# Cross-attention and a LoRA mixture on one core: the context's means through device memory, scores in 512-column matmuls, and the fifth tile turned by TensorE

## What is computed

```python
# _layernorm: (x - mean) / sqrt(var + 1e-5)
scores  = einsum('bsd,bmd->bsm', layernorm(x), ctx) / 32       # 64 context rows per batch
attn    = softmax(where(mask, scores, -1e30))
x       = x + einsum('bsm,bmd->bsd', attn, ctx)                # zero where no row is valid
n       = layernorm(x)
base    = n @ weight.T                                         # 1024 x 1024
probs   = softmax(n @ router_w.T)                              # 8 experts; the two best, renormed
expert  = sum over e of w[e] * ((n @ lora_A[e].T) @ lora_B[e]) * 2   # rank 16
x       = x + base + expert
```

## Time and profile before

| | |
|---|---|
| median of 3 runs | 1054.0 us (1053.96 to 1054.96) |
| the profiled execution's own time | 1054.39 us |
| its span, first to last instruction | 1052.3 us |
| granted TensorE clock | 1.0 over the whole span |
| TensorE busy | 1043.5 us, 99% |
| VectorE busy | 817.3 us, 78% |
| ScalarE busy | 477.7 us, 45% |
| GpSimd busy | 147.8 us, 14% |
| DMA | 149 GB/s in the mean |

### The profile page before, as it was taken

How to read it: one execution, slowest core, us unless ns; L and a number is a source line. 1 busy time by engine, 2 the same in 40 slices (tenths; PEclk the granted TensorE clock), 3 DMA queues, 4 the chain that set the end, 5 groups by cost and what they waited for, 6 DMA issues and landing times.

```text
span 1052.3 us, 18830 instructions
## 1 busy us (share of the span) xinstructions
PE 1043.5 (99%) x6078; PEld 1028.7 (98%) x6078; DVE 817.3 (78%) x2203; ACT 477.7 (45%) x929; POOL 147.8 (14%) x278
## 2 busy tenths in 40 slices
PE   8999999999999999999999999999999999999998
PEld 7999999999999999999999999999999999999998
DVE  6987887788777887878877888778888778777663
ACT  7754544445434544444444345344444444443320
POOL 3211211111111111111111111111111111111100
PEclk9999999999999999999999999999999999999999
DMA  8555556654556555475545655455654565554431
GB/s 306 201 160 124 149 154 163 170 147 122 149 158 179 143 123 142 143 201 131 152 115 150 185 149 150 135 132 171 163 150 137 118 174 153 152 149 114 114 75 58
DMA packets 157248, 156.81 MB, mean 149 GB/s; under 512 B 95120, under 2 KB 130064, under 8 KB 157200
## 3 DMA queue, kind: packets, MB, share of 16 engines
q1 hardware_dynamic: 156336, 154.82, 53.9%
q10 hardware_dynamic: 864, 1.45, 0.4%
HBM read 78.74 MB, written 33.55 MB: 107 GB/s over the span
## 4 chain that ended last, share of the span: by engine, by line
PE 95%; DVE 2%; DMA 1%; POOL 0%; issue 0%; ACT 0%; SPq 0%; ACTq 0%; DVEq 0%; POOLq 0%
PE base_ps L1086 28%; PE base_ps L1088 28%; PE base_ps L1087 28%; PE ro_ps L1150 3%; PE s_ps L1114 3%; PE ro_ps L1151 3%; PE s_ps L1113 3%; DMA xT_raw<-in_xT 1%; DVE stats L885 0%; DVE w_lo L331 0%; DVE x_first L879 0%; SPq L374 0%; DVE xT_lo L801 0%; DMA w_raw<-w_raw 0%; SPq L410 0%
## 5 line engine op out<-in xcount | busy, mean ns | idle before, releaser
L1086 PE MATMUL base_ps<-w_hi,xT_hi 128*128 128x388 f32 x1512 | 513.7, 340 | 0.0
L1088 PE MATMUL base_ps<-w_hi,xT_lo 128*128 128x388 f32 x1512 | 512.5, 339 | 0.0
L1087 PE MATMUL base_ps<-w_lo,xT_hi 128*128 128x388 f32 x1512 | 511.4, 338 | 0.0
L1087 PEld LDWEIGHTS base_ps<-w_lo,xT_hi 128*128 128x128 f32 x1512 | 284.7, 188 | 2.8
L1086 PEld LDWEIGHTS base_ps<-w_hi,xT_hi 128*128 128x128 f32 x1512 | 284.0, 188 | 2.7
L1088 PEld LDWEIGHTS base_ps<-w_hi,xT_lo 128*128 128x128 f32 x1512 | 284.3, 188 | 0.0
L487 POOL TENSOR_TENSOR rstd<-var_eps,neg_half 128x1 f32<-128x1 f32 x64 | 65.3, 1020 | 567.7 <-DVE var_eps L892 567.7
L901 DVE STREAM_TRANSPOSE x2T<-xq 128x512 f32<-128x512 f32 x122 | 121.5, 1072 | 5.3 <-DMA xq<-xn 4.7
L605 ACT CAST xT_hi<-x2T 128x512 fp32r<-128x512 f32 x122 | 69.6, 618 | 85.3 <-DVE x2T L901 85.3
L916 DVE MAX8 top<-base_ps 128x8 f32<-128x8 f32 x64 | 11.2, 174 | 106.8 <-PE base_ps L1088 106.8
L599 ACT ACTIVATE xn<-w_raw,shift,rstd 128x1024 f32<-128x1024 f32 x32 | 39.9, 1245 | 94.1 <-POOL shift L490 94.1
(11 more groups left out here) (128 smaller groups left out, 1382.5 us busy)
## 6 DMA issues: line engine op xcount, KB each, us to landing
xT_raw<-in_xT SPq DMA_DIRECT2D x62, 512.0 KB, 5.3
xq<-xn SPq DMA_DIRECT2D x244, 128.0 KB, 3.6
w_raw<-in_x SPq DMA_DIRECT2D x32, 512.0 KB, 3.5
out<-x_first SPq DMA_DIRECT2D x32, 512.0 KB, 2.7
out<-w_raw SPq DMA_DIRECT2D x31, 512.0 KB, 2.7
x_first<-in_x SPq DMA_DIRECT2D x30, 512.0 KB, 3.5
h<-w_raw SPq DMA_DIRECT2D x248, 16.0 KB, 1.9
w_raw<-w_raw SPq DMA_DIRECT2D x120, 32.0 KB, 1.9
```

The source lines that it names most:

```text
L1086: pe.matmul(out_, a_hi, w_h, start=start, stop=False, skip_group_check=again)
L1087: pe.matmul(out_, a_hi, w_l, start=False, stop=False, skip_group_check=again)
L1088: return pe.matmul(out_, a_lo, w_h, start=False, stop=stop, skip_group_check=again)
```

## The change

Three edits, and what they bring along.

1. **Means by row sums.** From the second batch on `ctx_mean` and `ctx_sum_chunks` are gone. VectorE sums each context row over its 1024 numbers (`ctx_row_sum`, step 3, in front of `s_transposes`); SyncE stores the 128 sums to a small tensor in device memory and loads them back, spread over all partitions (in step 2 of its own order, around `s_exchange`); `ctx_centre` subtracts them in two instructions of 256 elements, in place. `ctx_low` moves on VectorE from step 5 to step 6, in front of the router.
2. **Wide scores.** High and low parts of `xT` lie in one tensor, and a block of the contraction takes one matmul of 512 columns in place of two of 256. The two halves are no longer added in PSUM: VectorE adds them with a `tensor_reduce` (`s_sum`) and turns the sum. TensorE's wait before `pair_scores` is on that sum.
3. **The fifth tile.** Tile (0, 4) takes the path of the first four: its scores and exponentials are turned by TensorE. Tile (0, 5) has its scores turned by TensorE, and its exponentials by VectorE as before. SyncE's exchanges for them fall away, and the order around them in the start is changed.

```diff
 # SyncE, step
-                if exists(after(tile, 3)) and not first:
+                if exists(after(tile, 3)) and not first and not turned_on_pe(after(tile, 3), 5):
                     e_exchange(after(tile, 3))
...
-                if j % 2 == 0 and exists(after(tile, 4)):
+                if j == 2 and exists((b, TPB)):
+                    sp.wait_ge(row_sum_done, b + 1)
+                    sp.dma_start(ctx_rows, row_sum[:, :]).then_inc(row_sum_stored, 16)
+                if j % 2 == 0 and exists(after(tile, 4)) and not first:
                     s_exchange(after(tile, 4))
+                if j == 2 and exists((b, TPB)):
+                    sp.wait_ge(row_sum_stored, b * 16 + 16)
+                    sp.dma_start(row_sums[:, :], ctx_rows.rearrange("q o -> o q").to_broadcast([P, P]))\
+                      .then_inc(row_sums_loaded, 16)
 # ScalarE, start
             norm1_squares((0, 4))
+            sT_copy((0, 4))
 # VectorE
+            def ctx_row_sum(b):
+                dve.wait_ge(ctx_loaded, b * 16 + 16)
+                dve.tensor_reduce(out=row_sum[:, :], in_=ctx_raw[:, 0:D], axis=AX.X, op=ALU.add).then_inc(row_sum_done, 1)
+
             def ctx_centre(b):
-                dve.wait_ge(ctx_mean_done, b + 1)
-                dve.tensor_tensor(ctxT_centred[:, :, :], ctxT_raw[:, :, :],
+                dve.wait_ge(ctxT_loaded, b * 16 + 16)
+                dve.wait_ge(row_sums_loaded, b * 16)
+                for j in range(2):
+                    keys = ctxT_raw[:, :, j * QP:(j + 1) * QP]
+                    sums = row_sums[:, :].rearrange("p (r j) -> p j r", j=Q)[:, j]
+                    dve.scalar_tensor_tensor(out=keys, in0=sums.unsqueeze(1).to_broadcast([P, C, QP]), scalar=-1.0 / D,
+                                             in1=keys, op0=ALU.mult, op1=ALU.add).then_inc(ctx_centred, 1)
...
             def s_transposes(tile):
                 dve.wait_ge(sT_done, pairs(tile, 1, 1))
+                dve.tensor_reduce(out=s_sum, in_=s_ps[:, :].rearrange("p (l t) -> p t l", l=2), axis=AX.X,
+                                  op=ALU.add).then_inc(s_sum_done, 1)
+                dve.wait_ge(s_sum_done, pairs(tile, 1, 1 - 3))
                 dve.transpose(sq.rearrange("p (j k c) -> p k j c", k=2, c=QP),
-                              s_ps[:, 0:T2].rearrange("p (k j c) -> p k j c", k=2, c=QP)).then_inc(sq_done, 1)
+                              s_sum.rearrange("p (k j c) -> p k j c", k=2, c=QP)).then_inc(sq_done, 1)
...
+                if j == TPB - 2 and exists((b, TPB)):
+                    ctx_low(dve, b + 1)
                 router_top(tile)
...
+                if j == TPB - 5 and exists((b, TPB)):
+                    ctx_row_sum(b + 1)
                 if j % 2 == 1 and exists(after(tile, 3)):
                     s_transposes(after(tile, 3))
...
-                if j == TPB - 3 and exists((b, TPB)):
-                    ctx_low(dve, b + 1)
...
             add_readout((0, 3))
-            s_transposes((0, 4))
             norm2_stats((0, 3))
             norm2_moments((0, 3))
+            first_softmax_scores((0, 4))
             add_bases((0, 1))
-            softmax_scores((0, 4))
 # TensorE
                 pe.wait_ge(xT_split, pairs(tile, 2, 2))
+                for c in range(C):
+                    mm = pe.matmul(s_ps[:, 0:2 * T2], ctxT[:, c, :], xT_parts[:, :, :, c, :], start=(c == 0), stop=(c == C - 1))
+                mm.then_inc(sT_done, 1)
...
                 base(tile, 0, range(C))
-                if j == TPB - 4 and exists((b, TPB)):
-                    ctx_mean(b + 1)
-                base(tile, 1, range(C))
+                base(tile, 1, range(HC))
+                if turned_on_pe(nxt2, 5):
+                    e_transpose(nxt2)
+                base(tile, 1, range(HC, C))
...
                 base(tile, 2, range(C))
+                if turned_on_pe(after(tile, 3), 6):
+                    scores(after(tile, 3))
...
-            pair_scores((0, 4))
+            first_pair_scores((0, 4))
             base((0, 1), 2, range(7, C))
+            scores((0, 4))
```

More of the change, by code:

```diff
@@ L94, in exists, with turned_on_pe @@
         return not isinstance(tile[0], int) or tile[0] * TPB + tile[1] < NT
+    def turned_on_pe(tile, n):
+        return isinstance(tile[0], int) and tile[0] * TPB + tile[1] < n
     def slot(tile):
@@ L406, in e_exchange @@
             def e_exchange(tile):
-                sp.wait_ge(eq_done, count(tile, 1, 1 - 4))
+                sp.wait_ge(eq_done, count(tile, 1, 1 - 5))
                 for i in range(Q):
@@ L412, in s_exchange @@
             def s_exchange(tile):
-                sp.wait_ge(sq_done, pairs(tile, 1, 1 - 2))
+                sp.wait_ge(sq_done, pairs(tile, 1, 1 - 3))
                 for i in range(Q):
@@ L526, in ctxT_high @@
             def ctxT_high(b):
-                act.wait_ge(ctx_centred, b + 1)
-                act.copy(ctxT[:, :, 0:M], ctxT_centred[:, :, :]).then_inc(ctxT_hi_done, 1)
+                act.wait_ge(ctx_centred, b * 2 + 2)
+                act.copy(ctxT[:, :, 0:M], ctxT_raw[:, :, :]).then_inc(ctxT_hi_done, 1)
             def ctx_high(b):
@@ L571, in softmax_exp @@
                 act.wait_ge(softmax_step, count(tile, 5, 3))
-                act.wait_ge(eq_done, count(tile, 1, -4))
+                if turned_on_pe(tile, 6):
+                    act.wait_ge(eT_done, count(tile, 1))
+                else:
+                    act.wait_ge(eq_done, count(tile, 1, -5))
                 act.activation(e_all[:, :], s_all[:, :], ACT.Exp, bias=neg_max[:, :],
@@ L577, in eT_copy @@
             def eT_copy(tile):
-                act.wait_ge(e_loaded, count(tile, 16 * Q, 16 * Q * (1 - 4)))
+                act.wait_ge(e_loaded, count(tile, 16 * Q, 16 * Q * (1 - 5)))
                 act.wait_ge(readout_done, count(tile, 2))
@@ L819, in softmax_scores @@
                 dve.wait_ge(rstd1_done, count(tile, 1, 1))
-                dve.wait_ge(s_loaded, pairs(tile, 16 * Q, 16 * Q * (1 - 2)))
+                dve.wait_ge(s_loaded, pairs(tile, 16 * Q, 16 * Q * (1 - 3)))
                 dve.scalar_tensor_tensor(out=by_blocks(s_part[:, :]), in0=s_raw[:, 2:4, k, :], scalar=rstd1[:, :],
@@ L1000, in step @@
                     norm2_moments(nxt2)
-                if j == TPB - 3 and exists((b, TPB)):
-                    ctx_low(dve, b + 1)
                 if exists(nxt):
                     x2T_low(nxt)
-                if j == TPB - 5 and exists((b, TPB)):
-                    ctx_sum_chunks(b + 1)
                 if j == TPB - 4 and exists((b, TPB)):
                     ctxT_low(b + 1)
-                if exists(after(tile, 3)):
+                if turned_on_pe(after(tile, 3), 6):
+                    first_softmax_scores(after(tile, 3))
+                elif exists(after(tile, 3)):
                     softmax_scores(after(tile, 3))
@@ L1017, in _ @@
             dve.wait_ge(constants_ready, CONSTANTS)
-            ctx_sum_chunks(0)
-            ctx_centre(0)
+            first_ctx_sum()
+            first_ctx_centre()
             first_xT_low(0, 0)
@@ L1203, in step @@
                 base(tile, 0, range(C))
-                if j == TPB - 4 and exists((b, TPB)):
-                    ctx_mean(b + 1)
-                base(tile, 1, range(C))
+                base(tile, 1, range(HC))
+                if turned_on_pe(nxt2, 5):
+                    e_transpose(nxt2)
+                base(tile, 1, range(HC, C))
                 if j % 2 == 1 and exists(after(tile, 3)):
-                    pe.wait_ge(sq_done, pairs(after(tile, 3), 1, -2))
+                    if not turned_on_pe(after(tile, 3), 7):
+                        pe.wait_ge(s_sum_done, pairs(after(tile, 3), 1, -3))
                     pair_scores(after(tile, 3))
@@ L1340 @@
     out = nc.dram_tensor("out", (B * S // P, P, O), mb.dt.float32, kind="ExternalOutput").ap()
-    xattn_lora_moe_kernel(nc, *args, out)
+    rows = nc.dram_tensor("ctx_rows", (P, 1), mb.dt.float32, kind="Internal").ap()
+    xattn_lora_moe_kernel(nc, *args, out, rows)
     r = run_bass_kernel_spmd(nc, [{f"in_{n}": a for n, a in arrays.items()}], core_ids=[0])
```

53 lines of the change are left out of this document (35 added, 18 removed).

## The result

The changed kernel takes 1065.28 us in the median of four runs (1063.07 to 1066.62), the kernel before 1054.22 in its four: ratio 1.0098, 95% interval 1.0086 to 1.0110. That is 11 us slower. The forecast was 1054.6 with a range up to 1058.0; the time lies outside it, and of the cases named only C and D lie on its side.

The account below looks back on a forecast made before the run. TensorE was taken as the bound, never waiting in the steady part. Sure gains of 2.4 us against 1.6 for late landings and 1.4 for the centring gave +0.6: 1054.6 us on the median, range 1051.3 to 1058.0.

Parts of the forecast that it names:

- Rival C: VectorE's sum of the halves takes over 1.3 us: about 1062 us at 1.5, 1081 at 2.3; chance 0.20.
- Rival D: Row sums return late from device memory, VectorE stands at the centring: 1066 us if 2 us over; chance 0.04.
- The trip through device memory: SyncE's store and load of the row sums land 1.9 us after issue, leaving 6 us; cost 0.
- The mean's matmul: Its removal from TensorE saves 0.22 us a batch, 1.5 us in seven batches, as a sure gain.
- Wide scores: TensorE's 512-column score matmuls gain 0.02 us a pair, 0.6 us in 29 pairs.
- The start: Fifth tile: 1.0 us wait gone, less 0.4 for turns and 0.25 waiting; gain 0.3 us (0 to 0.6).
- The sum of the halves: VectorE's new reduce from PSUM takes 1.08 us (bounds 0.68 and 2.3), so later work slips by 0.96 us.
- The centring: VectorE's two instructions before eT in step 4, 0.42 or 0.6 us each; costs 0.3 to 2.4 us, taken as 1.4.
- Late landings at even readouts: VectorE's slip makes TensorE wait for eT in three of 13 even steps; 1.6 us over 15 steps.

Follow-up runs that it names:

- e3: Changed kernel without the store of the row sums and the wait for it; the load reads the context input instead: 1053.90 us, ratio 0.9996.
- e7: Kernel of e6 with a store of 64 bytes per partition in place of four, same number of pieces: 1054.80 us, ratio 1.0006.
- e6: Changed kernel with the four-byte store kept but no SyncE wait for it; the load reads the context input: 1069.41 us, ratio 1.0153.
- e9: Changed kernel with the sums turned by VectorE, so the store is four DMAs of 128 bytes: 1053.66 us, ratio 0.9996.
- e4: Changed kernel with s_exchange issued before the store, SyncE still waiting for the store's landing: 1102.66 us, ratio 1.0461.
- e1: Changed kernel with the means made by matmul as before, the other edits kept: 1053.46 us, ratio 0.9993.
- e13: Kernel of e9 with the store behind s_exchange, the load behind e_exchange in SyncE's step 3, centring at the end of step 4: 1052.40 us, ratio 0.9983.
- e2: Kernel before with the means by row sums alone, narrow scores and old path of the fifth tile: 1068.14 us, ratio 1.0136.
- e11: Kernel before with an unused tensor of four bytes per partition in front of ctx_sum: 1055.70 us, ratio 1.0015.
- e12: Kernel before with the wide scores alone, same size of all tensors: 1055.16 us, ratio 1.0010.
- e5: Kernel of e1 with later SBUF tensors at their addresses of the kernel before (old tensor back, row-sum tensors out): 1052.28 us, ratio 0.9984.
- e8: Changed kernel with store and load issued by ScalarE and the centring one place later: 1064.32 us, ratio 1.0095.

## Why the prediction was wrong

**The step that failed** is "The trip through device memory": "Small DMAs land 1.9 us after issue. So 6 us are left. Cost 0". The 1.9 us came from copies inside SBUF in pieces of 256 bytes. The store is 128 pieces of four bytes, and it lands after 7.7 us, its load after 4.5. That alone would still have fitted: by the prediction's own times there were 12.8 us from the store (471.7) to the centring (484.5), and 7.7 + 4.5 is 12.2. What I didn't ask is what stands behind the store: `s_exchange`, and SyncE's exchanges for the next tile. e3 (no store: 11 us back), e7 (larger pieces: 15 us less than e6) and e9 (whole change, rows of 128 bytes: 12 us back) show the cause; e6 and e4 show its two ways apart, since e6 has no wait on SyncE and is slow by the held exchange, and e4 has the exchange ahead and is slow by the wait. In the changed kernel it is the first: e6 loses no less than it does.

The Trainium skill says of this ("DMA: Bandwidth & Descriptors", "Specifications") that under 512 bytes a DMA engine reads, changes and writes back, and gives 512 as the least transfer for full rate. I had read past it. Here pieces of 64 bytes (e7) and 128 bytes (e9) do no harm, so what the runs show is less than that rule: four bytes are ruinous, 64 are not. Between them nothing was tried, and how closely the pieces lie went with their size.

**Rival D** had the right object and the wrong place: in the changed kernel VectorE does not stand at the centring but at the scores' exchange. Its chance of 0.04 was far too small. That its 1066 us (sums 2 us late) lie so near the measured 1065.3 is luck: the sums were not late in the changed kernel. **Rival C** is refuted: the reduce takes 0.69 us, and e1 has it without loss.

**The mean's matmul.** Right: 0.22 us per batch, 15.26 to 15.03 in e13.

**Wide scores.** I had 0.02 us a pair, it is 0.05 (16.97 to 16.92). In all 1.4, not 0.6.

**The start.** I had 0.3; tile 3 starts 0.7 to 1.4 us earlier in the kernels that have the third edit's path, and from 0.4 us earlier to 0.05 later in e2, e11 and e12, which don't. So some 0.9 is the edit's and the rest differs from run to run. The 0.25 I allowed for the turn of the scores was not there: in the changed kernel TensorE's distances around it are 0.27 and 0.09, so the turn takes the 0.18 that it costs and no wait.

**The sum of the halves.** 0.69 us, my lower bound. The stride of 256 numbers costs nothing where the source is PSUM. The Trainium skill's smaller lines of PSUM ("SBUF — State Buffer", "Door 1: The DMA port swizzle") spoke for a penalty; for VectorE the measurement decides. **The centring** took nearly the slow bound, 0.58 each where 0.42 was reckoned without a penalty; I put that down to the stride of four numbers read from SBUF, which was not tried apart. I had 1.4 us for it in the middle of two bounds; e3's 0.28 in seven batches is 2.0.

**Late landings at even readouts.** The mechanism is real and shows in e12. For the changed kernel I had 1.6 us for it; with 0.69 us for the sum the working gave 0.3. In e5 steps (1, 2) and (0, 6) are long by 0.35 and 0.27 (the latter already 0.14 in the kernel before), together about 0.5.

So without the store the time would have come near the sum: e3 has 1053.9 us and e9, the whole change with another store, 1053.7, where I had said 1054.6. In part that is luck. Wide scores (1.4 for 0.6), the start (0.9 for 0.3) and the late landings (0.5 for 1.6) came out better than I had them, by 2.5 us; the centring (2.0 for 1.4) came out worse, and e3 also has some 1.5 us (measured in e11) for the place of the tensors in SBUF, which stood in no term. What stays open: why the store of four-byte pieces takes so long and holds the other transfers (the runs show only that both queues suffer), and why e13 and e5 tie though e13 has no mean on TensorE. By steps, e13 is 0.23 ahead in each of the later steps (b, 4), and loses as much in three steps of batches 0 and 1; I didn't follow these. So no run shows that the means by row sums gain anything over the matmul: the best kernel with them (e13, 0.9983 of the time before) and the best without (e5, 0.9984) are equal.

## What to carry to other kernels

Price a DMA by a row with the same piece size and the same kind of target, and where there is none, treat the transfer as unknown, however few bytes it has. Ask of each new DMA not only who waits for it but what lands behind it: a slow one holds up those of other queues too. When TensorE is the bound, a gain in its instructions is kept only if the small exchanges that feed the next tile keep their slack. And a long wait can cost more than its own length: look at the granted clock behind it.

## What was not expected of the hardware

- A store of 128 pieces of 4 bytes to device memory lands after 7.7 to 8.2 us in the median (after, e2, e4, e6, e8). Exchanges issued by another queue land after up to 6.8 us in place of 1.9, and VectorE waits for them up to 4.7 us (e8); 128 pieces of 64 bytes land after 2.9.
- Four bytes of shift of the SBUF tensors behind a pad cost TensorE 0.055 us in each step without scores: e11 has 15.09 against 15.03. At the same time DMAs land sooner: `xq` in 3.1 us against 3.6 in the median, and the DMA share between 447 and 1030 us falls from 0.54 to 0.47 at the same 144 GB/s. With a shift by 1280 bytes (e9) all three are as before: 15.03, 3.6 and 0.54. The cause was not looked for.
- After seven waits of 4.5 to 5.3 us (e4) TensorE's granted clock was at 0.50 (1.2 GHz) for 3 to 6 us each time. In the changed kernel it fell likewise once, behind a wait of 2.06 us; waits up to 1.69 us there, and one of 2.2 us in e2, left it at 1.00.
- VectorE reads pairs 1 KB apart in PSUM at the rate of neighbours (690 ns for 512).
